# One transformer layer on one core: attention scores made once, in row tiles, instead of twice

## The reference, cut to what matters

```
x: (4, 512, 512)   Wqkv: (512, 1536)   Wo: (512, 512)   w1, w3: (1365, 512)   w2: (512, 1365)

y      = layernorm(x)
q,k,v  = split(y @ Wqkv) into 16 heads of 32
scores = q k^T * 32**-0.5, masked with -1e9 above the diagonal
x      = x + (softmax(scores) v) @ Wo
z      = layernorm(x)
x      = x + (silu(z @ ternary(w1)^T) * (z @ ternary(w3)^T)) @ ternary(w2)^T
```

## Time and profile before

| what | value |
|---|---|
| runs | 572.34 us median, 571.48 to 573.64 |
| profiled execution: its own time, as the span of the profile | 570.0 us |
| TensorE busy | 540.9 us (95%) |
| VectorE busy | 373.7 us (66%) |
| ScalarE busy | 265.0 us (46%) |
| GpSimd busy | 289.8 us (51%) |
| DMA | 58.52 MB, 38.8% of 16 engines' span |
| instructions | 8957 |

### The profile page before, as it was taken

How to read it: one execution, slowest core, us unless ns; L and a number is a source line. 1 busy time by engine, 2 the same in 40 slices (tenths; PEclk the granted TensorE clock), 3 DMA queues, 4 the chain that set the end, 5 groups by cost and what they waited for, 6 DMA issues and landing times.

```text
span 570.0 us, 8957 instructions
## 1 busy us (share of the span) xinstructions
PE 540.9 (95%) x3180; PEld 252.7 (44%) x3180; DVE 373.7 (66%) x937; ACT 265.0 (46%) x437; POOL 289.8 (51%) x339
## 2 busy tenths in 40 slices
PE   3899789999999999999999999999989999999997
PEld 3444334344444445444444444444434444444443
DVE  7797798988986766615786757565774645554421
ACT  4877688848263636232353635431235743013320
POOL 5152799687544558400747284701448787113320
PEclk9999799999999999999999999999999999999999
DMA  8979969677852030035573012214230001150001
GB/s 330 321 166 264 215 173 249 181 164 153 176 140 73 1 93 21 1 93 148 131 127 97 18 36 59 75 37 132 74 57 1 3 0 56 38 129 1 0 20 55
DMA packets 82880, 58.52 MB, mean 103 GB/s; under 512 B 51434, under 2 KB 71914, under 8 KB 82836
## 3 DMA queue, kind: packets, MB, share of 16 engines
q1 hardware_dynamic: 82836, 57.95, 38.8%
HBM read 33.55 MB, written 12.58 MB: 81 GB/s over the span
## 4 chain that ended last, share of the span: by engine, by line
PE 63%; POOL 11%; DVE 10%; DMA 6%; ACT 4%; SPq 3%; issue 3%; DVEq 0%; ACTq 0%
PE work L1092 38%; PE work L1272 13%; PE score_bank L1167 4%; PE prob_bank L1189 3%; POOL early L650 3%; PE work L1210 3%; POOL early L641 2%; POOL early L653 2%; DMA early<-in_L_ffn_w 2%; ACT early L755 2%; PE work L1232 2%; DVE masked L954 2%; DVE rows L929 1%; POOL early L675 1%; DMA late<-rows 1%
## 5 line engine op out<-in xcount | busy, mean ns | idle before, releaser
L1092 PE MATMUL work<-late,w_ternary 128*128 128x512 f16 (+1 forms) x704 | 160.4, 379 | 1.3 <-DMA late<-rows 0.8
L755 ACT ACTIVATE early<-prob_bank,scalars 128x512 f32<-128x512 f32 x160 | 100.3, 683 | 98.6 <-PE prob_bank L1189 98.4
L954 DVE CUSTOM_DVE_ANT_0 masked<-score_bank,mask 128x512 f16<-128x512 f32 (+3 forms) x256 | 111.6, 485 | 26.6 <-PE score_bank L1167 26.2
L1092 PEld LDWEIGHTS work<-late,w_ternary 128*128 128x128 f16 (+1 forms) x704 | 68.9, 100 | 77.6 <-issue 2.2
L667 POOL TENSOR_TENSOR late<-late 128x512 f16<-128x512 f32 (+1 forms) x44 | 50.6, 1157 | 60.2 <-ACT late L775 60.2
L641 POOL TENSOR_SCALAR_AFFINE_SELECT early<-early 128x640 f32<-128x640 f32 (+2 forms) x96 | 43.7, 486 | 72.9 <-ACT early L755 72.9
L1272 PE MATMUL work<-w_ternary,late 128*128 128x512 f16 (+1 forms) x352 | 78.0, 379 | 0.0
L990 DVE SCALAR_TENSOR_TENSOR late<-late,work 128x512 f32<-128x512 f32 (+1 forms) x44 | 30.2, 686 | 52.3 <-ACT late L768 52.2
L1092 PE MATMUL work<-xt,wqkv_hi 128*128 128x512 f16 x192 | 57.2, 380 | 2.6 <-DVE wqkv_lo L909 1.4
L650 POOL TENSOR_TENSOR early<-early 128x768 f32<-128x768 f32 x32 | 58.4, 1826 | 2.0
L1167 PE MATMUL score_bank<-k_stack,q_stack 96*128 96x512 f16 (+3 forms) x256 | 51.0, 305 | 4.9 <-DMA k_stack<-k_lo_spill 2.5
(11 more groups left out here) (112 smaller groups left out, 761.0 us busy)
## 6 DMA issues: line engine op xcount, KB each, us to landing
rows<-in_L_attn_x SPq DMA_DIRECT2D x16, 256.0 KB, 3.0
q_stack<-q_hi_spill SPq DMA_DIRECT2D x32, 128.0 KB, 2.6
k_stack<-k_hi_spill SPq DMA_DIRECT2D x32, 128.0 KB, 3.0
x_res<-in_L_attn_x SPq DMA_DIRECT2D x12, 256.0 KB, 3.0
out_y<-x_res SPq DMA_DIRECT2D x12, 256.0 KB, 2.2
late<-in_L_ffn_w SPq DMA_DIRECT2D x4, 682.5 KB, 4.4
early<-in_L_ffn_w SPq DMA_DIRECT2D x3, 768.0 KB, 12.2
late<-in_L_ffn_w SPq DMA_DIRECT2D x3, 768.0 KB, 4.9
```

Of the source, the lines that this page charges most:

```text
L755: act.activation(probs[:, u, :], prob_bank[u % 2][:], ACT.Exp, scale=scalar(exp_scale)).then_inc(prob_free, 1)
L954: dve.tensor_tensor_reduce(masked[:, k % 2, 0:n], score_bank[u % 2][:, off:off + n], mask[:, S - n:S], 1.0, LOWEST, ALU.add, ALU.max, row_ ...
L1092: last = pe.matmul(bank, lhs, rhs, start=(n == 0), stop=(n == len(terms) - 1))
```

## The change

Scores are made once. The stacks, the spills, the turned maxima and the second score product are gone. For each head the score is made from the three pairs of halves with 32 rows each, at the head's own 32 partitions of the array, four heads in four banks one after the other (a row tile of 32). A slot is three "fills" of the four score banks: row tile 3 (512 keys), row tiles 2 and 0 (384 + 128), row tile 1 (256). VectorE scales, masks, takes the maximum and writes the f32 result out to `raws` (four buffers, so one per head); GpSimd makes the exponent's bias from two heads' maxima; ScalarE exponentiates in place with that bias and adds up the row as it goes; VectorE (or for some fills ScalarE, `high`) makes the high f16 half, GpSimd the low half (`low`); a transposing transfer on SP's queue (`probs_turn`) turns both halves of four heads, 32, 32 and 16 blocks of 128x128 f16. `values` then works with f16 halves in three terms. The sums are inverted in 128x16 values and spread by TensorE (`inverse`, 16 small f32 matmuls). The low halves of `xt` and `yt` move from VectorE to GpSimd; v is split in halves too; `warm` steps are gone; x_res is loaded at the start.

```diff
@@ constants
-NW = 4
-WARM = 4
-STACKS = 3
+HALVES = 3
+RAWS = 4
+FILLS = (((3, 0, 512),), ((2, 0, 384), (0, 384, 128)), ((1, 0, 256),))
@@ sync
-            def stack(s):
-            def max_row(step):
...
+            def probs_turn(s, p):
+                fill = NF * s + p
+                if fill == 0:
+                    sp.wait_ge(turned["w1"], 16 * len(TURNS["w1"]))
+                if s:
+                    full(sp, ("values", s - 1))
+                sp.wait_ge(low_done, HG * (fill + 1))
+                sp.dma_start_transpose(probs[:, TURNED_AT[p]:TURNED_AT[p] + BLOCKS[p], :],
+                                       split_probs[fill % 2][:, 0:BLOCKS[p] * P]).then_inc(probs_turned[fill % 2], 16)
@@ gpsimd
-            def select(s, pair):
-            def add(s, pair):
...
+            def low(s, p, h):
...
+                pool.tensor_tensor(split_view(s, p, 1, h), raw_view(s, p, h), split_view(s, p, 0, h),
+                                   ALU.subtract).then_inc(low_done, 1)
+            def bias(s, p, h):
...
+                pool.wait_ge(score_free, place(s, p, h) + 1)
+                pool.tensor_scalar(exp_bias[:, (NF * s + p) % 2, both], row_max[:, (NF * s + p) % 2, both], -1.0, LOG_UNIT,
+                                   ALU.mult, ALU.add).then_inc(bias_made, 1)
@@ scalar
-                    act.activation(probs[:, u, :], prob_bank[u % 2][:], ACT.Exp,
-                                   scale=scalar(exp_scale)).then_inc(prob_free, 1)
+                for j, (tile, off, cols) in enumerate(FILLS[p]):
...
+                    last = act.activation(piece, piece, ACT.Exp, bias=bias, accum_out=sums[:, s % 2, at:at + 1])
+                last.then_inc(exp_done, 1)
@@ vector
+            def maxima(s, p, h):
...
+                dve.wait_ge(score_full, fill + 1)
+                if n >= RAWS:
+                    dve.wait_ge(low_done, n - RAWS + 1)
...
+                    last = dve.tensor_tensor_reduce(raws[n % RAWS][:, off:off + cols], score_bank[h][:, off:off + cols],
+                                                    mask[:, S - cols:S], scalar(exp_scale), LOWEST, ALU.add, ALU.max,
+                                                    row_max[:, fill % 2, first + j:first + j + 1])
+            def high(s, p, h):
...
+                dve.tensor_copy(split_view(s, p, 0, h), raw_view(s, p, h)).then_inc(high_done["dve"], 1)
@@ tensor
+                for j, (tile, off, cols) in enumerate(FILLS[p]):
+                    for t, (a, b) in enumerate((("hi", "hi"), ("hi", "lo"), ("lo", "hi"))):
+                        for h in range(HG):
+                            if fill and j == t == 0:
+                                pe.wait_ge(score_free, HG * (fill - 1) + h + 1)
+                            heads = slice(HD * h, HD * (h + 1))
+                            last = pe.matmul(score_bank[h][:, off:off + cols],
+                                             half["q", a][s % HALVES][heads, tile * P:(tile + 1) * P],
+                                             half["k", b][s % HALVES][heads, 0:cols], start=(t == 0), stop=(t == 2))
@@ the end of the lists "pe"
-        values:14 sums:14 probs:15,0 gate:2,7 probs:15,1 lin:2,7 probs:15,2 gate:2,8 lin:2,8 probs:15,3 gate:2,9
-        probs:15,4 lin:2,9 gate:2,10 values:15 lin:2,10 sums:15 down:2,0-1 project:3,0-3 down:2,2-3 gate:3,0
+        lin:2,10 values:14 down:2,0 scores:15,2 down:2,1-2 inverse:15 down:2,3 values:15 project:3,0-3 gate:3,0-1
```

709 lines of the change are left out of this document (337 added, 372 removed).

## The result

The changed kernel takes 579.25 us (median of four runs, 577.75 to 580.78) against 572.65 (571.48 to 573.64): 1.0109 times as long, 95% interval 1.0084 to 1.0134. Forecast was 566. The profiled execution has a span of 579.0, 9.0 more than before.

The account below looks back on a forecast made before the run. TensorE was taken to bound stages 2 to 5, with stage 1 shared and passing to VectorE and ScalarE. Stage 1 at 158 plus 406 gave a 564 span, 566 us against 572.3; 8-in-10 range 541 to 594.

Parts of the forecast that it names:

- I take 158: Stage 1, up to the first gate: 158 us against 167.4 before, with ends of 145 and 176.
- The rate: Stage 1: the fuller of VectorE and ScalarE stays 86% busy, as now, which gives 162 us.
- I count it at nothing: TensorE's fills waiting on VectorE's maxima and GpSimd's low halves: round 4.5 to 5 us, 8 to 10 between fills, nothing added.
- VectorE's work: Stage 1: VectorE busy 139 us instead of 143.2, with maxima saving 13 and high-half copies adding 38.
- Attention starts some 20 us earlier: Stage 1: the first attention fill no longer waits for w1's turned weights, which helps to fill VectorE and ScalarE.
- Transfers hidden: Stage 1: transposing transfers at 0.13 us a block bring DMA to 147 of 158 us, tight but counted as hidden.
- Row tiles together: TensorE's scores: four heads run beside each other, 1.65 us per slot against 6.6 if none do, plus 1.1 overhead.
- The lost cover: End of stage 4: no down steps before batch 3's gate; waits of 9.5+0.5 and 2.5, cooling 2.3, together 14.8 us.
- Rival 2: VectorE copies and GpSimd subtractions hold each other up: stage 1 at 172, 12 us of later waits, 592 total; chance 0.15.
- Rival 3: Transfers bound stage 1 at 0.155 us a block: stage 1 at 174, the whole at 582; chance 0.1.
- Rival 4: Row tiles of the scores run one after another: 54 us instead of 13, total 607; chance 0.05.
- Rival 1: List laid for the new loads, denser: stage 1 at 145, half the overhead, tail of 9, total 540; chance 0.25.

Follow-up runs that it names:

- The run on the kernel before: Kernel before the change, with batch 2's last two down steps moved ahead of batch 3's first project: 584.07 us, 1.0197 times as long.

## Why the prediction was wrong

The direction was missed: 566 forecast, 579 measured. Stage 1 missed by 22.1 us, and stages 2 to 5 together gave 7.1 back.

- **"I take 158" for stage 1** is the step that failed, with three parts. (1) *The rate.* The fullest engine was to be 86% busy. VectorE is at 145.1 of 180.1, 81%: by that alone 169 becomes 180. A busy sum over five queues does not see a ring in which each step waits for the one before; "I count it at nothing", on the added wait, is where the ring was dropped. I had set its 5 us (its terms add up to 4.3 to 4.7) against 8 to 10 between fills, but that spacing is TensorE's in stages 2 to 4; in stage 1 nothing else fills the time, and a fill took 7.8 us, with roundings, row splits and the transfer of two fills before queued in it. (2) *VectorE's work*, 145 instead of 139: 7 us at 86%. The copies, which I had doubted, came out as forecast: 63 of them in stage 1 took 39.4 us, 0.65 in the mean, where I had 38 (those of 512 columns took 0.76, those of 256 only 0.40). The term that was too small is the maxima. I priced them as before the change, 7.0 us a slot; as the change has them (scaling as well, and writing f32 and not f16) they take 131.7 us over 16 slots, 8.2 a slot. In stage 1 they fell from 50.9 to 44.6 us, by 6.3 and not by 13. (3) *"Attention starts some 20 us earlier"* was misread (4 us in the forecast). The first scores do not wait for w1, but the first transfer and the second fill's copies do, and values of slot 0 come 5.9 us later than before. 4+7+11 = 22, but this is a way to divide the miss and no three measurements: the 81% holds the late start too. VectorE is idle for 35.0 us of stage 1 against 24.2 before, 2.7 of the 10.8 more up to 55 us and 8.1 behind it.
- **Transfers hidden.** 147 us of DMA time forecast for stage 1, 164 measured, 0.18 us a block. Halving them alone is worth 1.9 us, so hidden was nearly right, until low halves are halved too.
- **ScalarE 134 and GpSimd 123** came out at 126.3 and 125.6, the accumulator reads at 0.19 each. TensorE's 100 us of work were 126.9 busy: at a mean granted clock of 0.85, where stage 1 had 0.98 before.
- **Row tiles together**: right. Stages 2 and 3 were 7.0 us shorter than forecast. The waits that I took over from the old lists, 6.0 us, were 1.3 (0.8 and 0.4 of idle TensorE); the other 2.3 say that the overhead was some 0.8 us a slot and not 1.1.
- **The lost cover**: right in mechanism and size. 10.3 us ahead of the gate (9.5+0.5 forecast), 2.85 ahead of project (2.5), 2.6 in stage 5 at the lower clock (2.3). The run on the kernel before prices it alone at 11.7 us of span. Giving the steps back to the changed kernel returns 3.7, as the last slot's transfers then stand open.
- **Rival 2** named the right mechanism for stage 1: VectorE's copies and GpSimd hold each other up, and the round has a part in it. But it needed copies of 0.9 us, and they took 0.65 in the mean, within the forecast's 0.5 to 0.7; it had the stage at 172 and 12 us of waits in stages 2 to 4, where TensorE waits for nearly nothing. Its test (score matmuls wait over 10 us for VectorE) came true at 20.6 us, all in stage 1. **Rival 3** came near the total (582) by a cause that is worth 1.9 us alone. **Rival 4** is ruled out by the rows of scores. **Rival 1** took the list as well laid; it wasn't, in the start (4.3 us) and the tail (3.7).
